# Second layer: values times keys as four matmuls of 32 by 32 in place of two of 64 by 64

## The chip, the cores and the metric

The kernel runs on one core of one Trainium2 chip. The metric is the device time of one execution in microseconds (us), and of several runs the median. Times of single instructions are in nanoseconds (ns).

## What is computed

Two layers of linear attention on x of shape (8, 512, 512), one after the other, each with its own weights. Cut to what matters, with H = 8 heads of 64 features in the first layer and H = 16 heads of 32 features in the second:

```
xn = layernorm(x)
q, k, v = xn @ Wq + bq, xn @ Wk + bk, xn @ Wv + bv      # masked by token
q = softmax(q, over the features of a head)
k = softmax(k, over the tokens)
attn = einsum('bhse,bhsd->bhed', k, v)                  # per head
y = einsum('bhtd,bhed->bhte', q, attn)                  # second layer
h = layernorm(y) * (1 + scale) + shift                  # scale, shift from silu(emb) @ W_emb
x = x + silu(h) @ W_out + b_out
```

(The first layer multiplies y the other way round, 'bnhd,bhdl->bnhl'.) The change touches the line of `attn`, in the second layer. Per batch entry and head it is a matrix of 32 by 32 there, summed over 512 tokens.

## The kernel before

**Units.** The work is cut into 16 units, one per layer and batch entry: units 0 to 7 are the first layer, 8 to 15 the second. Each unit has 512 tokens in four tiles of 128, and 512 features in four chunks of 128. Every product is made of float16 parts: a number is split into a high and a low part, and a product is high times high, high times low and low times high, so that each chunk of a sum is three matmuls (`split_pairs`).

**Order.** All orders are written out by hand, one list per engine, in functions `step(u)` for units 1 to 14 and `last_unit` for 15. TensorE does in unit u: keys K(u), values V(u), queries Q(u), each 48 matmuls of 512 columns (`project_keys`, `project_tokens`, all recorded at L534); then `attention(u)`, the product of values and keys (L658), into the PSUM bank `att_ps`; then the output projection of the unit before, `output(u - 1)`, 48 matmuls at L534; then `attend(u)`, queries times that product (L709), 96 matmuls. Unit 15 has the queries ahead of the values and the output tiles of unit 14 around `attention` and `attend`.

**The product of values and keys.** `attention(u)` walks over four chunks c of 128 features. A chunk holds two heads of the first layer or four of the second; heads don't mix, so of the 128 by 128 product of a chunk only blocks on the diagonal are wanted. `pairs_of_heads` makes, for each of the 12 pairs of operands (four token tiles by three parts), two matmuls: j = 0 takes the first 64 features of both operands and writes partitions 0 to 63, j = 1 the other 64 and partitions 64 to 127. That is 12 by 2 by 4 = 96 matmuls per unit, each with its weight load, all 128 rows deep. In the second layer a block of 64 by 64 holds two heads and, off its diagonal, two blocks of 32 by 32 that no head wants; `mask_attention` on DVE (L1089 in the second layer) multiplies by a table of blocks that is zero there, adding a value column first, and writes `att`. ACT and POOL split `att` into `att_hi` and `att_lo`, which `attend` reads.

**What waits for what around it.** TensorE starts `attention(u)` when the transposed keys, the low parts of the values and the gate of the unit before are ready. DVE does in unit u: four key tiles (`masked_keys`, L864 and L1021; L864 is a small memset that carries the wait for the tile) in between the work on the hidden rows of the unit before; low parts of keys; low parts of values (L1052); four query tiles (`queries`, L1072, L1075, L1077); `mask_attention`; sums; four residuals (L1120), each when an output tile is done; and the work on y (`attended_all`, L1130 to L1147), when `attend` has done two tiles. ACT takes the exponent of the queries (L1497) and their high part (L1504), POOL their low part (L1714).

**SP's queue.** SP issues the DMA transposes (L410), in this order in a unit: keys, h, the first half of the next unit's x, queries high and low (`turn_q`), the second half of the next unit's x (`turn_x(u, 1)`). `attend(u)` waits for the transposed queries, K(u + 1) for the transposed x. The queue is strictly in order.

Of the kernel before, what the change touches and what calls it, by code (L numbers as in the profile page):

```python
# [5 lines left out]
P = 128  # L6
# [10 lines left out]
HALF = P // 2  # L17
# [32 lines left out]
def layer_of(u):  # L50
    return u // B
# [55 lines left out]
def build(nc, x_d, emb_d, mask0_d, mask1_d, w_d, bias_d, wemb_d, cols_d, ident_d, blocks_d, out_d):  # L107
    with ExitStack() as ctx:
# [105 lines left out]
        def tile(buffer, a, b):  # L214
            return buffer[:, (4 * a + b) * P:(4 * a + b + 1) * P]
# [29 lines left out]
        def att_count(u):  # L245

            return C + u + (C - 1 if u == LAST else 0)
# [271 lines left out]
        def _(pe):  # L519
# [17 lines left out]
            def split_pairs(lhs_hi, lhs_lo, rhs_hi, rhs_lo):  # L537
                return [p for c in range(C) for p in ((lhs_hi(c), rhs_hi(c)), (lhs_hi(c), rhs_lo(c)), (lhs_lo(c), rhs_hi(c)))]
# [111 lines left out]
                    last = nc.tensor.matmul(out, ones[:], rows, start=True, stop=True)  # L650
                last.then_inc(shift_summed, 1)

            def pairs_of_heads(c, pairs):

                for n, (lhs, rhs) in enumerate(pairs):
                    for j in range(2):
                        g = slice(j * HALF, j * HALF + HALF)
                        last = nc.tensor.matmul(att_ps[g, c, g], lhs[:, g], rhs[:, g], start=(n == 0), stop=(n == len(pairs) - 1))  # L658
                return last

            def attention(u):
                pe.wait_ge(kt_hi_ready, 16 * (u + 1))
                pe.wait_ge(kt_lo_ready, 16 * (u + 1))
                pe.wait_ge(v_lo_ready, 4 * (u + 1))
                if u:
                    pe.wait_ge(att_ready, att_count(u - 1))
                if u == 2:
                    pe.wait_ge(film_copied, 4)
                for c in range(C):
                    f = slice(c * P, c * P + P)  # L670
                    k_parts = (lambda t: tile(kt_hi, c, t), lambda t: tile(kt_lo, c, t))
                    v_parts_t = (lambda t: v_hi[:, t, f], lambda t: v_lo[:, t, f])
                    left, right = (k_parts, v_parts_t) if layer_of(u) == 0 else (v_parts_t, k_parts)
                    last = pairs_of_heads(c, split_pairs(*left, *right))
                last.then_inc(att_summed, 1)

            def first_attention(between):
# [69 lines left out]
            def step(u):  # L747
# [34 lines left out]
                if shifted is not None:  # L782
                    pe.wait_ge(shift_folded, folded(1, shifted))
                pe.wait_ge(h_ready, 4 * u)
                attention(u)
                if u == 1:
                    pe.wait_ge(o0_ready, 1)
# [7 lines left out]
            def last_unit(u):  # L795
                pe.wait_ge(xt_hi_ready, 32 * u)
                pe.wait_ge(xt_lo_ready, 32 * u)
                project_keys(u)
                project_tokens("Q", u, Q_, xt_hi, xt_lo)
                project_tokens("V", u, V_, xt_hi, xt_lo)  # L800
                pe.wait_ge(ht_hi_ready, 16 * u)
                pe.wait_ge(ht_lo_ready, 16 * u)
                output(u - 1, (0,))
                pe.wait_ge(h_ready, 4 * u)
                attention(u)
                output(u - 1, (1,))
                attend(u)
                output(u - 1, (2, 3))
# [1043 lines left out]
```

## Time and profile before

| | |
|---|---|
| three runs | 805.05, 800.82, 802.58 us |
| median | 802.58 us |
| profiled execution, span from first to last instruction | 799.5 us |
| instructions in the trace | 16864 |
| DMA, mean over the span | 164 GB/s |

For the profiled execution no time of its own is given beside its span, so what lies around the span is taken from the median: 3.1 us. The profile is one execution. TensorE has two rows in it: PE is the matmuls, PEld the weight loads, which overlap them. A row such as "128*64 128x64 f16 x96" reads: weights of 128 rows by 64 columns, moving operand of 128 rows by 64 columns, float16, 96 of them merged. Matmuls are pipelined, so the duration of one (196 ns here) is not its cost: the cost is the distance from one start to the next. "issue" is time in which an engine waited for nothing that the profile shows; the landing of a DMA transpose is among what it does not show. SPq is the queue of SP: its rows give the time that issuing takes, not the landing.

### The profile page before, as it was taken

How to read it: one execution, taken by the hardware profiler on the slowest of the kernel's cores; microseconds unless marked ns; L12 is line 12 of the kernel's file. 1: busy time of each engine (PE TensorE's matmuls, PEld its weight loads, DVE VectorE, ACT ScalarE, POOL GpSimd, SP SyncE). 2: the span in 40 equal slices, each digit the busy share in tenths (PEclk: the TensorE clock that was granted, in tenths of full speed). 3: DMA queues.
4: the chain of work that ended last, by engine and by line, in shares of the span. 5: the costliest groups of instructions: out<-in, count | busy, mean ns of one | idle time of the engine just before them, and what ended most of it. 6: DMA issues, size and time to landing. Idle time of an engine off the chain costs nothing.

```text
span 799.5 us, 16864 instructions
## 1 busy us (share of the span) xinstructions
PE 761.5 (95%) x6359; PEld 370.6 (46%) x6359; DVE 697.7 (87%) x1427; ACT 517.5 (65%) x1011; POOL 438.5 (55%) x433
## 2 busy tenths in 40 slices
PE   5997999999999999998999999999999999999986
PEld 2445444454544445444444544444454544444442
DVE  7898978798998999999988898898888889888885
ACT  5896766666667686885856685665767575560633
POOL 2465573663737767486672755447364545546323
PEclk9997999999999999999999999999999999999999
DMA  9976895856939769595794939487684939477462
GB/s 327 297 142 183 253 184 176 158 139 162 182 128 158 198 137 201 134 200 148 137 220 87 204 93 180 151 159 198 99 198 113 190 123 185 112 139 153 80 132 80
DMA packets 291249, 130.73 MB, mean 164 GB/s; under 512 B 261440, under 2 KB 261824, under 8 KB 291168
## 3 DMA queue, kind: packets, MB, share of 16 engines
q1 hardware_dynamic: 288432, 125.27, 70.8%
q10 hardware_dynamic: 2736, 4.39, 1.5%
q8 instruction: 50, 0.82, 0.4%
q14 instruction: 31, 0.25, 0.1%
HBM read 47.74 MB, written 16.88 MB: 81 GB/s over the span
## 4 chain that ended last, share of the span: by engine, by line
PE 85%; DVE 9%; issue 3%; ACT 2%; DMA 0%; POOL 0%; SPq 0%; DVEq 0%; ACTq 0%; POOLq 0%
PE ring L534 75%; PE ring L709 3%; PE att_ps L658 3%; DVE sb_k_or_qt L1042 1%; DVE sb_row_peak L881 1%; ACT sb_k_or_qt L1440 1%; DVE sb_q_sum L1101 1%; PE ring L834 0%; PE att_ps L595 0%; PE film_ps L595 0%; DVE sb_q_max L1075 0%; DVE ring L1072 0%; DVE sb_ht_parts L1158 0%; PE film_ps L604 0%; DMA sb_x<-in_x 0%
## 5 line engine op out<-in xcount | busy, mean ns | idle before, releaser
L534 PE MATMUL ring<-sb_w_hi,sb_xt_parts 128*128 128x512 f16 x1024 | 309.0, 379 | 0.0
L534 PE MATMUL ring<-sb_w_lo,sb_xt_parts 128*128 128x512 f16 x512 | 194.0, 379 | 0.0
L534 PE MATMUL ring<-sb_w_hi,sb_ht_parts 128*128 128x512 f16 x512 | 155.8, 379 | 4.0 <-ACT sb_ht_parts L1610 1.4
L534 PEld LDWEIGHTS ring<-sb_w_hi,sb_xt_parts 128*128 128x128 f16 x1024 | 100.4, 98 | 126.0 <-issue 6.6
L534 PE MATMUL ring<-sb_xt_parts,sb_w_hi 128*128 128x512 f16 x496 | 148.6, 381 | 9.7 <-issue 9.1
L1698 POOL TENSOR_TENSOR sb_htok<-sb_ht_parts,sb_htok 128x512 f16<-128x512 f32 x60 | 75.0, 1272 | 137.8 <-ACT sb_htok L1473 137.8
L1714 POOL TENSOR_TENSOR sb_tanh<-sb_v_or_q,sb_kq_hi 128x512 f16<-128x512 f32 x64 | 74.1, 1159 | 87.7 <-ACT sb_kq_hi L1504 87.1
L534 PE MATMUL ring<-sb_w_lo,sb_ht_parts 128*128 128x512 f16 x256 | 97.0, 379 | 0.0
L534 PE MATMUL ring<-sb_xt_parts,sb_w_lo 128*128 128x512 f16 x248 | 94.5, 381 | 0.0
L1497 ACT ACTIVATE sb_v_or_q<-ring,sb_ln_one 128x512 f32<-128x512 f32 x64 | 43.9, 686 | 61.0 <-DVE ring L1077 60.9
L1689 POOL TENSOR_TENSOR sb_x<-sb_x,sb_bias_o 128x512 f32<-128x512 f32 x64 | 79.3, 1274 | 5.9 <-DVE sb_w_lo L958 5.9
L534 PEld LDWEIGHTS ring<-sb_w_hi,sb_ht_parts 128*128 128x128 f16 x512 | 50.1, 98 | 63.4 <-ACT sb_ht_parts L1610 4.1
L534 PEld LDWEIGHTS ring<-sb_xt_parts,sb_w_hi 128*128 128x128 f16 x496 | 47.5, 98 | 67.2 <-issue 12.3
L534 PEld LDWEIGHTS ring<-sb_w_lo,sb_xt_parts 128*128 128x128 f16 x512 | 50.1, 98 | 59.4 <-issue 0.7
L1709 POOL TENSOR_TENSOR sb_tok<-sb_v_or_q,sb_tok 128x512 f16<-128x512 f32 x56 | 66.4, 1199 | 17.1 <-ACT sb_tok L1436 17.1
L1417 ACT ACTIVATE sb_v_parts<-sb_x,sb_x_minus 128x512 f16<-128x512 f32 x52 | 36.9, 710 | 58.4 <-POOL sb_x_minus L1670 58.4
L1120 DVE SCALAR_TENSOR_TENSOR sb_x<-ring,sb_down_o,sb_x 128x512 f32<-128x512 f32 x60 | 43.2, 748 | 28.3 <-PE ring L534 26.0
L1042 DVE SCALAR_TENSOR_TENSOR sb_k_or_qt<-sb_k_or_qt,sb_k_recip,sb_kq_hi 128x512 f16<-128x512 f32 x64 | 61.5, 961 | 5.1
L1440 ACT ACTIVATE sb_k_or_qt<-sb_k_or_qt,sb_k_shift 128x512 f32<-128x512 f32 x64 | 45.4, 710 | 20.3 <-DVE sb_k_shift L1029 20.3
L1432 ACT ACTIVATE sb_v_or_q<-sb_x,sb_x_add,sb_x_rstd 128x512 f32<-128x512 f32 x56 | 43.9, 808 | 22.2 <-POOL sb_x_add L1677 22.2
L1464 ACT ACTIVATE att_ps<-sb_ht_parts,sb_scale_down 128x512 f32<-128x512 f32 x30 | 20.6, 687 | 57.6 <-DVE sb_ht_parts L1153 57.5
L1072 DVE SCALAR_TENSOR_TENSOR ring<-ring,sb_scale_down,sb_bias_q 128x512 f32<-128x512 f32 x64 | 48.0, 750 | 9.1 <-PE ring L534 9.0
(232 smaller groups left out, 1401.0 us busy)
## 6 DMA issues: line engine op xcount, KB each, us to landing
out<-sb_x SPq DMA_DIRECT2D x14, 1024.0 KB, 4.9
sb_rows_now<-film_rows SPq DMA_DIRECT2D x16, 512.0 KB, 4.5
sb_x<-out SPq DMA_DIRECT2D x8, 1024.0 KB, 5.2
sb_x<-in_x SPq DMA_DIRECT2D x7, 1024.0 KB, 5.4
sb_mask_add<-mask_terms SPq DMA_DIRECT2D x15, 256.0 KB, 5.5
sb_w_hi<-in_L_cond_W_emb SPq DMA_DIRECT2D x1, 1536.0 KB, 14.1
sb_w_lo<-in_L_cond_W_emb SPq DMA_DIRECT2D x1, 1536.0 KB, 14.4
sb_w_hi<-in_L_cond_film_emb_W ACTq DMA_DIRECT2D x1, 1536.0 KB, 11.9
```

The source lines that it names most:

```text
L534: last = nc.tensor.matmul(out, lhs, rhs, start=(n == 0), stop=(n == len(pairs) - 1))
L1042: nc.vector.scalar_tensor_tensor(out=k_lo[:, i * S:i * S + S], in0=k_or_qt[:, i, :], scalar=k_recip[:, i:i + 1], in1=kq_hi[:, i * S:i * S ...
L1072: nc.vector.scalar_tensor_tensor(out=here, in0=here, scalar=scale_down[:, layer, Q_:Q_ + 1], in1=bias_q[layer][:], op0=ALU.mult, op1=ALU.a ...
L1120: nc.vector.scalar_tensor_tensor(out=xt(unit, t), in0=bank("O", t, unit), scalar=down_o[:, layer:layer + 1], in1=xt(unit, t), op0=ALU.mult ...
L1417: nc.scalar.activation(unused(unit)[:, t, :], xt(unit, t), ACT.Square, bias=x_minus[:, t:t + 1], accum_out=x_square[:, t:t + 1]).then_inc( ...
L1432: nc.scalar.activation(xh_of(unit)[:, t, :], xt(unit, t), ACT.Identity, bias=x_add[:, t:t + 1], scale=x_rstd[:, t:t + 1]).then_inc(xh_read ...
L1440: nc.scalar.activation(k_or_qt[:, i, :], k_or_qt[:, i, :], ACT.Exp, bias=k_shift[:, i:i + 1], accum_out=k_sum[:, i:i + 1]).then_inc(k_exp, 1)
L1497: nc.scalar.activation(q[:, t, :], bank("Q", t, u), ACT.Exp, bias=ln_one[:]).then_inc(q_exp, 1)
L1689: nc.gpsimd.tensor_tensor(xt(u, t), xt(u, t), bias_o[layer][:], ALU.add).then_inc(x_biased, 1)
L1698: nc.gpsimd.tensor_tensor(hp_lo[:, t, :], y_of(unit)[:, t, :], hp_hi[:, t, :], ALU.subtract).then_inc(h_lo_ready, 1)
L1709: nc.gpsimd.tensor_tensor(xp_lo[:, t, :], xh_of(unit)[:, t, :], xp_hi[:, t, :], ALU.subtract).then_inc(xp_lo_ready, 1)
L1714: nc.gpsimd.tensor_tensor(q_lo[:, t * D:t * D + D], q[:, t, :], kq_hi[:, t * D:t * D + D], ALU.subtract).then_inc(q_lo_ready, 1)
```

## The change

In units 8 to 15 each group of two matmuls of 64 by 64 becomes a group of four matmuls of 32 by 32, one per head, in the four quarters of the array's columns, with outputs in the four quarters of the partitions. A unit's block has 12 by 4 by 4 = 192 matmuls and as many weight loads in place of 96. The blocks off the heads' diagonal are no longer written; the table of blocks zeroes them as before. Units 1 to 7 call the same function with two groups, and unit 0 has its own (`first_attention`). Nothing else changes: in the order of TensorE's instructions each row of 96 matmuls of 64 by 64 in units 8 to 15 is a row of 192 of 32 by 32 at the same place, with the same waits. The new function is one line longer, so that lines behind it have numbers higher by one in the changed kernel.

```diff
-            def pairs_of_heads(c, pairs):
-
+            def groups_of_features(c, groups, pairs):
+
+                width = P // groups
                 for n, (lhs, rhs) in enumerate(pairs):
-                    for j in range(2):
-                        g = slice(j * HALF, j * HALF + HALF)
+                    for j in range(groups):
+                        g = slice(j * width, j * width + width)
                         last = nc.tensor.matmul(att_ps[g, c, g], lhs[:, g], rhs[:, g], start=(n == 0), stop=(n == len(pairs) - 1))
                 return last
...
-                    last = pairs_of_heads(c, split_pairs(*left, *right))
+                    last = groups_of_features(c, 4 if layer_of(u) else 2, split_pairs(*left, *right))
```

## Rows read from the trace of the kernel before

**Rows 1.** The page: busy time by engine, and the ending chain by engine
```profile
PE 761.5 (95%) x6359; PEld 370.6 (46%) x6359; DVE 697.7 (87%) x1427; ACT 517.5 (65%) x1011; POOL 438.5 (55%) x433
...
PE 85%; DVE 9%; issue 3%; ACT 2%; DMA 0%; POOL 0%; SPq 0%; DVEq 0%; ACTq 0%; POOLq 0%
```

**Rows 2.** Chain of waits, units 8 to 15: start us, us, what
```profile
456.21 0.82 issue
457.03 31.24 PE ring L534 x144
...
502.55 1.01 issue
...
548.42 0.31 issue
...
593.58 0.49 issue
...
638.92 0.75 issue
...
684.53 0.12 issue
...
729.79 1.20 issue
...
769.82 1.67 issue
```

**Rows 3.** Stretches, L658 alone: length, PE, PEld, clock, DMA share, GB/s
```profile
442.53:444.17 1.64, 1.64 (x96) 1.59 (x96) 1.00 1.39 248
...
sum 13.12, PE 13.12 PEld 12.75; mean PE 1.64 PEld 1.59
```

**Rows 4.** PE in order, unit 8; first only up to 443.0 us
```profile
442.53 0.66 PE L658 MATMUL att_ps<-sb_kt_or_y,sb_v_parts 128*64 128x64 f16 x30
...
442.22 0.38 PE L534 MATMUL ring<-sb_w_hi,sb_xt_parts 128*128 128x512 f16 x1
442.53 1.71 PE L658 MATMUL att_ps<-sb_kt_or_y,sb_v_parts 128*64 128x64 f16 x96
...
445.26 0.59 PE L534 MATMUL ring<-sb_w_hi,sb_ht_parts 128*128 128x512 f16 x2
```

**Rows 5.** SP queue in order, transposes, units 9, 10, 11, 14
```profile
498.43 3.20 SPq L410 DMA_TRANSPOSE sb_xt_parts<-sb_tok  x2
...
543.60 3.19 SPq L410 DMA_TRANSPOSE sb_xt_parts<-sb_tok  x2
...
589.21 2.89 SPq L410 DMA_TRANSPOSE sb_xt_parts<-sb_tok  x2
...
725.70 3.18 SPq L410 DMA_TRANSPOSE sb_xt_parts<-sb_tok  x2
```

**Rows 6.** DVE in order: fourth key tile, units 9 to 15; L1089
```profile
467.69 0.06 DVE L864 MEMSET sb_spare<- 128x1 f32 x1 [0.91 <-PE ring L534]
...
491.69 1.12 DVE L1089 SCALAR_TENSOR_TENSOR sb_att<-att_ps,sb_v_column_up,sb_blocks 128x128 f32<-128x128 f32 x4
...
514.22 0.06 DVE L864 MEMSET sb_spare<- 128x1 f32 x1 [0.17 <-PE ring L534]
...
559.75 0.06 DVE L864 MEMSET sb_spare<- 128x1 f32 x1
...
605.22 0.06 DVE L864 MEMSET sb_spare<- 128x1 f32 x1
...
650.33 0.06 DVE L864 MEMSET sb_spare<- 128x1 f32 x1 [0.85 <-PE ring L534]
...
695.91 0.06 DVE L864 MEMSET sb_spare<- 128x1 f32 x1
...
741.64 0.06 DVE L864 MEMSET sb_spare<- 128x1 f32 x1 [0.71 <-PE ring L534]
```

**Rows 7.** The page, DMA queues: packets, MB, share of 16 engines
```profile
q8 instruction: 50, 0.82, 0.4%
```

## The prediction

> **What bounds the kernel now.** I read the page first [rows 1]: TensorE is busy 95% of the span and the chain that ended last lies on it for 85%, which looks as if every microsecond taken from it were a microsecond gained. The chain of waits of units 8 to 15 then corrects that [rows 2]. In each of units 8 to 14 TensorE stands still behind the last product of queries and attention (L709), before the next unit's keys: 0.82, 1.01, 0.31, 0.49, 0.75, 0.12 and 1.20 us, all "issue", a wait whose end the profile does not name. The queue of SP names it [rows 5]: the last pair of transposes of the next unit's x is issued until 501.63, 546.79, 592.10 and 728.88 us in units 9, 10, 11 and 14, and the next keys start at 503.56, 548.73, 594.07 and 730.99 (a piece of rows 2 plus its length), 1.93, 1.94, 1.97 and 2.11 us later. So the keys start when a transpose lands. These transposes stand on SP behind those of the queries, and those wait for DVE, ACT and POOL on the query tiles, which come from the Q projection ahead of the changed block. The block is no link of that chain.
>
> The block (L658) itself takes 1.64 us in each unit, 13.12 us for the eight units of the second layer [rows 3], at a granted clock of 1.00, the 2.4 GHz level. DVE takes its result (L1089) in unit 9 at 491.69 us [rows 6], 1.85 us after it is there (488.20 plus 1.64), because four query tiles stand ahead of it.
>
> There is a second way from the block to the end: block, output projection, L709, then DVE's work on y, behind which DVE takes the four key tiles of the next unit. The fourth tile of units 9 and 10 comes 10.66 us after the first key matmul (467.69 less 457.03, 514.22 less 503.56), and DVE waits for it 0.91 and 0.17 us; 0.85 in unit 13 and 0.71 in unit 15 [rows 6]. In units 11, 12 and 14 there is no wait: DVE starts at 559.75, 605.22 and 695.91 where the tile was there at 559.39, 604.73 and 695.31, so DVE is late by 0.36, 0.49 and 0.60 us. Only there does an earlier block help. DVE then runs on to the queries and so to SP's transposes, and its gain is kept to the end.
>
> **The change, part by part.** Units 0 to 7 keep their matmuls. In eight units a block of 96 matmuls (48 pairs of two 64 by 64) becomes one of 192 (48 groups of four 32 by 32), each with its weight load; waits, order and DMAs stay, apart from more instructions to fetch.
>
> Price of a group. In the block 66 matmuls take 1.71 less 0.66 us [rows 4], 15.9 ns each, 31.8 a pair. 64 columns at 2.4 GHz are 26.7 ns, which leaves 5.1, or 2.6 for each matmul. In the projections 144 matmuls of 512 columns take 31.24 us [rows 2], 217 ns each against 213 of columns, 3.6 each. No row has quarters of the columns with 32 moving columns. Bounds: 13.3 ns of columns and the same 5.1 give 18.4; two halves one behind the other, 63.6. Between them I take 13.3 and four times 2.6, 23.7 ns, since the pair of this line is the nearest row and already shows two matmuls that overlap. That is 8.1 ns a group and 48 groups: the block falls by 0.39 us, eight of them by 3.1 us.
>
> What of it counts. In units 8, 9, 12 and 14 the gain falls in front of units whose DVE waits for keys anyway (9, 10, 13, 15): nothing, TensorE's idle time grows. The blocks of units 10, 11 and 13 feed units 11, 12 and 14, where 0.36, 0.39 and 0.39 us count: 1.1 us. In unit 15 TensorE waits 1.67 us for the transposed queries ahead of the last L709 [rows 2], so a faster block there gives nothing. What is late next is in every unit the transpose of x.
>
> Here a rule of the Trainium skill speaks against the change: "TensorEngine Tiling (Array Packing)", Instruction Overhead, puts some 60 cycles on each matmul, so that fewer columns than that save nothing, and advises against cutting a dimension that is already small. The pairs do not contradict it if each tile of the array has this floor of its own; two matmuls in 31.8 ns do contradict one floor for all. The sum by it is a rival below.
>
> More instructions: q8 carries 0.82 MB in 50 packets [rows 7], which for 2 times 6359 instructions is 64 bytes each, 256 to a packet. 1536 more instructions in all are 768 more matmuls and as many loads: 0.1 MB and six packets, nothing for the DMA engines. A block is now 384 instructions and crosses at least one packet; cover is whatever is fetched ahead. I cost it at nothing; without cover it is a rival.
>
> Sum: the profiled span of 799.5 us less 1.1 is 798.4. The median of the runs shown lies 3.1 above this span, so 801.5 us. A measurement here can tell about 0.5%, 4 us, from no change.
>
> **Rivals.**
> 1. A floor per tile (the page's rule as a mechanism here): 60 of the 64 columns' time, 25 ns, and the same 5.1 make 30.1 ns a group, the block 0.08 us shorter, 0.24 us in three units: 802.3 us. For it: nothing in this trace streams fewer than 64 columns in f16. Against: nothing. 0.20.
> 2. No more than two matmuls overlap, so the rate of 15.9 ns for a matmul stays whatever its size: a group takes 63.6 ns and the block 1.53 us more. This is the rival on the other side. Unit by unit the delay is the larger of 1.53 less DVE's wait and 1.53 less TensorE's idle time: 0.71 (unit 9), 1.36, 1.53, 1.53, 0.78, 1.53, 0.82 (unit 15), together 8.3; the last block hides in 1.67. 810.9 us. In general the loss is seven times the growth of a block less 2.45 us, so it passes 4 us from 0.92 us a block on, a group of 51 ns. For it: 15.9 ns is the fastest rate of this line. Against: 26.7 of 31.8 ns are columns, so it is the columns that limit it. 0.09.
> 3. The instruction stream runs dry in the block: 384 instructions in 1.1 us against 192 in 1.6. A packet's time is 0.4% of 16 times 799.5 over 50, 1.0 us [rows 7]; a block longer by that on balance costs 7 less 2.45, 4.6 us: 807.2 us. Against: the bursts of today show no gap. 0.05.
> 4. Quarters do not overlap at all: four times 31.8, 127 ns; the block grows by 4.6 us, 29.6 us in seven units and 2.9 in the last: 835 us. 0.02.
> 5. The transposes follow TensorE after all, so that every unit passes the whole gain on, and a group takes 18.4 ns: eight times 0.64 us, 797.4 us. Against: the steady 1.9 to 2.1 us from SP's last issue to the keys. 0.04.
>
> **How the numbers follow.** The forecast has 0.60. It and rival 1 lie within 0.5%: 0.80. Slower by over 0.5% are rivals 2 to 4: 0.16; faster rival 5: 0.04. The range runs from 799.0 (the forecast, the runs' spread, no group below 18.4 ns) to 807.5 and takes in rival 3; left out are rivals 2, 4 and 5, 0.15.
>
> **What would show it.** Right: the stretch of L658 in units 8 to 15 is 1.2 to 1.3 us, rows of 192; the idle time ahead of the keys of units 9, 10, 13 and 15 grows by 0.3 to 0.4 us; SP's last issue is still 1.9 to 2.1 us ahead of the keys; DVE's lateness in units 11, 12 and 14 is gone or below 0.3. Wrong: a block at or above 1.6 us (rival 1 where it is 1.55, rivals 2 or 4 at 3.2 or 6), single gaps in the block beside a q8 packet (rival 3), or keys that start earlier against Q's end in every unit (rival 5).

## The result and the profile after

The changed kernel takes 822.41 us, median of five runs (819.56 to 824.34), against 802.58 us (800.82 to 805.05): the ratio is 1.0256, with a 95% interval of 1.0239 to 1.0273. It is 20 us slower, where 801.5 was forecast. Its profiled execution took 820.82 us, with a span of 819.0 us; before, the span was 799.5.

The page of the changed kernel, against [rows 1] and [rows 7]:

```profile
PE 768.9 (94%) x7127; PEld 372.2 (45%) x7127; DVE 697.7 (85%) x1427; ACT 517.8 (63%) x1011; POOL 438.1 (53%) x433
...
q8 instruction: 56, 0.92, 0.5%
...
PE 78%; DVE 12%; issue 5%; ACT 3%; DMA 0%; POOL 0%; DVEq 0%; SPq 0%; ACTq 0%; POOLq 0%
```

DVE, ACT and POOL do the same work in a longer span. There are 768 more matmuls and six more instruction packets, as counted ahead. In the chain "issue" rises from 3 to 5%. The chain of waits by time shows where it stands now, against [rows 2] (start us, us, what):

```profile
442.45 1.32 PE att_ps L659 x138
443.78 0.21 issue
443.99 0.57 PE att_ps L659 x54
...
487.79 1.60 PE att_ps L659 x167
489.40 4.02 issue
493.42 0.37 PE att_ps L659 x13
493.79 12.74 PE ring L534 x48
506.52 1.51 PE ring L710 x96
508.03 31.19 PE ring L534 x144
...
541.07 0.54 PE ring L534 x2
541.61 3.13 issue
...
587.51 1.79 PE att_ps L659 x192
589.30 10.47 PE ring L534 x48
...
681.70 2.95 issue
...
685.11 12.15 PE ring L534 x48
...
731.79 3.56 issue
...
735.62 12.99 PE ring L534 x48
```

The idle time ahead of the keys is gone in five of seven units (506.52 plus 1.51 is the start of the keys, 508.03). In its place TensorE stands still inside the block in units 8, 9, 13 and 14, two matmuls behind it in unit 10 and five behind it in unit 15, for up to 4 us, and the wait has no releaser in the profile. In unit 11 the same 192 matmuls pass without a stop.

The same places in TensorE's timeline, unit 9 and then unit 11:

```profile
487.72 1.68 PE L659 MATMUL att_ps<-sb_kt_or_y,sb_v_parts 128*32 128x32 f16 x167
493.42 0.37 PE L659 MATMUL att_ps<-sb_kt_or_y,sb_v_parts 128*32 128x32 f16 x25 [4.02 <-issue]
...
587.45 1.85 PE L659 MATMUL att_ps<-sb_kt_or_y,sb_v_parts 128*32 128x32 f16 x192
```

**What the stops have in common.** I numbered the records of TensorE's instructions in order of time, from the first one on. The first instruction behind each long stop has the number 193 or 194 modulo 256: in units 8, 9, 13 and 14 in the block, in units 10 and 15 a few matmuls behind it. A q8 packet is 0.92 MB over 56, 16.4 KB, 256 instructions of 64 bytes. So a stop lies at the edge of a packet. In the second layer the first edge inside a block comes at instruction 22, 79, 135, 192, 249, 50, 107 and 139 of the block in units 8 to 15, since a unit is 967 instructions long there, 57 short of four packets. The stop is always at the second edge, 256 instructions on. That fits a stream that can be two packets ahead, where the refill that starts at one edge must be there by the next.

| unit | first edge at | stop, us | from first edge to going on, us |
|---|---|---|---|
| 8 | 22 | 0.40 | 1.5 |
| 9 | 79 | 4.20 | 5.4 |
| 10 | 135 | 3.51 | 5.1 |
| 11, 12 | 192, 249 | none | |
| 13 | 50 | 3.14 | 4.3 |
| 14 | 107 | 3.74 | 5.1 |
| 15 | 139 | 2.28 | 4.4 |

(Here a stop is counted from one matmul's start to the next, 17.3 us in all.) A block of 384 instructions takes 1.7 us from its first matmul to its last where it does not stop (unit 11; 1.5 us before), and outruns the refill; one of 192 cannot hold two edges. In unit 8 the packet was under way 0.8 us ahead of the edge, while TensorE was still at the long matmuls in front of the block: I read this as the sequencer fetching ahead of the array. In the other units of the table the packet starts 1.8 to 3.1 us after the edge, takes 0.9 to 1.2 us, and TensorE goes on 1.4 us after its end.

A part of this price may belong to the DMA transposes. Around every block SP issues transposes: `turn_x` in units 9 to 14, those of the queries in unit 15. With them in flight the packets in the blocks start 1.8 to 3.1 us after the edge. Six other edges of the changed kernel in units 8 to 14 lie in the rows of L710, and there the packet starts 0.5 to 0.8 us after the edge, in four of them with no transpose packet in flight and in two with some. No run takes the transposes away, so what part of the price is theirs stays open.

The Trainium skill ("Runtime: NRT & Kernel Launch", Instruction fetch mechanics) has refills of 16 KiB, 256 instructions, into a memory of two such lines, and holds the fetch to be hidden since dispatch is slower than the refill. The trace agrees with the size and with two lines; here dispatch (256 instructions in about 1 us) was the faster one. The same section also gives TensorE 128 KiB, 2048 instructions, and with these stops the trace does not agree.

**The clock.** The stretches of unit 9 (length, PE, PEld, DVE, ACT, POOL busy, granted clock, DMA share, GB/s):

```profile
493.60:498.20 4.60, 4.60 (x36) 1.72 (x23) 4.26 (x10) 3.08 (x9) 3.13 (x4) 0.50 1.17 160
498.30:506.50 8.20, 8.20 (x42) 3.58 (x41) 2.71 (x5) 2.93 (x8) 5.00 (x7) 1.00 0.57 116
```

The granted clock falls inside the stop of 4.20 us, at 491.5, and is 0.50, the 1.2 GHz level, until 498.2, and then 1.00 again. The output projection takes 12.74 us in unit 9, 12.15 in unit 13 and 12.99 in unit 14 in place of 10.47. In unit 10, after a stop of 3.51 us, it did not fall. The lower clock adds 6.5 us to these three output projections.

**The sum of unit 9 closes.** Keys start later than before by -0.48, 4.47, 7.60, 8.30, 9.35, 14.12 and 19.12 us in units 9 to 15 (456.55 less 457.03, 508.03 less 503.56 and so on). The step of 4.95 us in unit 9 is: block and stop 6.00 in place of 1.64, 4.36; slower output tiles, 2.27; less the idle time of 0.60 ahead of L709 and of 1.01 ahead of the keys, both used up: 5.0.

Units 11 and 12 have no stop, and yet the keys behind them are a further 0.70 and 1.05 us late. For unit 12 the trace names a second way in which a refill costs time. Before, the transposes of x land 1.8 to 2.0 us after SP's last issue (the semaphore's times in the trace). SP's rows at the end of unit 12 are now:

```profile
642.70 2.78 SPq L410 DMA_TRANSPOSE sb_xt_parts<-sb_tok  x2
646.96 0.39 SPq L490 DMA_DIRECT2D out<-sb_x  x1
```

The last issue ends at 645.47, an instruction packet runs from 646.73 to 647.69, the transposes land at 648.93, 3.5 us after the issue, and the keys start at 649.02. Over all the kernels run here, nine of these landings ahead of the keys of units 9 to 15 took 3.1 to 3.6 us, and each of the nine had an instruction packet that started 0.6 to 1.5 us after SP's last issue. The other landings took at most 2.5 us, and four of them had such a packet too. So a packet seems able to hold a transpose up, but need not; no run was made for it.

### The profile page after: what moved, and what is told of

Its sections match the earlier page's. It is cut to its first block, busy times and chain, and to the rows that moved or that the text cites. A ratio compares the mean times of both kernels' runs of the same rounds, so it can differ in the third digit from the quotient of the medians.

```text
span 819.0 us, 18400 instructions
## 1 busy us (share of the span) xinstructions
PE 768.9 (94%) x7127; PEld 372.2 (45%) x7127; DVE 697.7 (85%) x1427; ACT 517.8 (63%) x1011; POOL 438.1 (53%) x433
## 4 chain that ended last, share of the span: by engine, by line
PE 78%; DVE 12%; issue 5%; ACT 3%; DMA 0%; POOL 0%; DVEq 0%; SPq 0%; ACTq 0%; POOLq 0%
PE ring L534 69%; PE att_ps L659 3%; PE ring L710 3%; DVE sb_k_or_qt L1043 1%; DVE sb_row_peak L882 1%; ACT sb_k_or_qt L1441 1%; DVE sb_q_sum L1102 1%; DVE sb_x L1121 1%; ACT sb_v_or_q L1488 1%; DVE ring L1131 1%; DVE sb_y_stats L1135 1%; DVE sb_ht_parts L1159 1%; ACT sb_v_parts L1490 1%; DVE ring L1073 1%; DVE sb_q_max L1076 1%
## 5 line engine op out<-in xcount | busy, mean ns | idle before, releaser
L534 PE MATMUL ring<-sb_w_hi,sb_ht_parts 128*128 128x512 f16 x512 | 160.6, 389 | 9.0 <-issue 6.1
L534 PE MATMUL ring<-sb_w_lo,sb_ht_parts 128*128 128x512 f16 x256 | 99.6, 389 | 0.0
```

Of the source, the lines that this page charges most:

```text
L534: last = nc.tensor.matmul(out, lhs, rhs, start=(n == 0), stop=(n == len(pairs) - 1))
```

## Experiments

**Shift the stream by 100 instructions.** Matmuls of 32 by 32 into the first bank of the keys, ahead of the keys of unit 8, 50 of them with their loads. Only the place of the packet edges changes for units 9 to 15.

```diff
+            def pad_keys(u, count):
+                out = take_bank("K", 0, u)
+                lhs, rhs = w_hi[1][K_][:, 0, 0:32], w_hi[1][K_][:, 1, 0:32]
+                for n in range(count):
+                    nc.tensor.matmul(out[0:32, 0:32], lhs, rhs, start=True, stop=True)
...
+                if u == B:
+                    pe.wait_ge(w_ready[1], 2)
+                    pad_keys(u, 50)
```

> Edit: the changed kernel, with 50 matmuls of 32 by 32 ahead of the keys of unit 8, into a bank that the keys then overwrite: 100 instructions more, once. Instructions come in packets of 256, and in the changed kernel the first packet edge inside a block of 384 lies at instruction 21, 76, 133, 190, 247, 48, 105, 138 of the block in units 8 to 15 (counted in the trace). Theory 'stream runs dry': TensorE stops where a second edge follows within some 5 us, that is where the first edge lies below about 140. Shifted by 100 the edges lie at 177, 232, 33, 90, 147, 204, 5, 38: long gaps (over 0.3 us) go from units 9 and 13 and appear in unit 11 (3 to 4.5 us); unit 10 shows a shorter one (0.4 to 3), unit 14 next to none, unit 15 one of 1 to 3. Time about 812 to 817 us. Rival 'quarters stall by themselves' (by place in the program or by their operands): the gaps stay in units 9, 10, 13 and 14, and the time is that of the changed kernel and 1.5 us, 822 to 826.

Measured: 815.67 us, ratio 1.0189 (1.0153 to 1.0226). TensorE's timeline, unit 9 and unit 11:

```profile
488.52 2.25 PE L665 MATMUL att_ps<-sb_kt_or_y,sb_v_parts 128*32 128x32 f16 x192
...
581.69 1.69 PE L665 MATMUL att_ps<-sb_kt_or_y,sb_v_parts 128*32 128x32 f16 x173
586.71 0.32 PE L665 MATMUL att_ps<-sb_kt_or_y,sb_v_parts 128*32 128x32 f16 x19 [3.32 <-issue]
```

The two units have changed places: unit 9 passes, unit 11 stops for 3.5 us at its instruction 347, where the edge was to lie. Units 13 and 14 have no long stop, unit 10 one of 0.8, unit 12 one of 1.5 us behind the block (edge at 148, which I had counted out), unit 15 one of 3.7, more than expected. The same instructions with the same operands stop or pass by their number alone.

**Keep the edge in a harmless place.** The same padding, 38 matmuls ahead of the keys of unit 8 and 29 ahead of those of each later unit, so that a unit is some 1024 instructions long.

> Edit: the changed kernel with 38 small matmuls ahead of the keys of unit 8 and 29 ahead of those of each unit 9 to 15, so that a unit is 1024 or 1025 instructions long and the packet edge stays at about instruction 200 of each block (170 in unit 15). Theory 'stream runs dry': no gap over 0.3 us in or behind any block, no fall of the granted clock, and a time of 802 to 806 us, since the added 0.5 us per unit lies mostly in the idle time ahead of the keys. Rival 'quarters stall by themselves': 820 to 828 us.

Measured: 805.7 us, ratio 1.0072 (1.0047 to 1.0096). The waits of TensorE in units 8 to 14 have one row left:

```profile
PE ring L716 <- issue: 0.4, 1, 0.4
```

and its chain of waits shows what the padding costs in each unit, here of units 10 and 11:

```profile
536.78 10.47 PE ring L534 x48
547.25 1.51 PE ring L716 x96
548.75 0.82 PE ring L657 x29
549.57 31.18 PE ring L534 x144
```

No stop, no slow output tile, all 1536 quarter matmuls still there, and some 15 of the 20 us are back (the ratio falls from 1.0256 to 1.0072). The 0.82 us of padding lie where TensorE idled before, and in four units they are more than that idle time, by 1.6 us together. The profiled execution agrees: its last keys come 1.7 us later than before. But it is the fastest of four, 803.49 us; the median is 5 us above before (4 to 8), and what the rest of these 5 us is stays open. It is still slower than the kernel before, and so no version to take.

**The old tiles, twice.** 384 instructions in a block, and no quarter among them: each chunk's 24 matmuls are issued twice.

```diff
-                    last = pairs_of_heads(c, split_pairs(*left, *right))
+                    for again in range(2 if layer_of(u) else 1):
+                        last = pairs_of_heads(c, split_pairs(*left, *right))
```

> Edit: the kernel before, with the 24 matmuls of each chunk issued twice in the second layer (the second time overwrites the first): 384 instructions in a block, all of the old 64 by 64 kind. The packet edges lie as in the changed kernel, but 256 instructions last 2.0 us in place of 1.0. 'Stream runs dry': gaps in or just behind the blocks of units 9, 10, 13, 14 and 15, each about 1 us shorter than in the changed kernel (2 to 3.3 us), and with the block 1.5 us longer a time of 822 to 830 us. Rival 'only quarters': no gap, and 1.0% above before.

Measured: 820.12 us, ratio 1.0248 (1.0227 to 1.0268), somewhat below the range expected. Unit 9:

```profile
489.19 2.85 PE L658 MATMUL att_ps<-sb_kt_or_y,sb_v_parts 128*64 128x64 f16 x167
495.01 0.60 PE L658 MATMUL att_ps<-sb_kt_or_y,sb_v_parts 128*64 128x64 f16 x25 [2.98 <-issue]
```

It stops at the same matmul as the changed kernel, the 168th. Stops of 3.18, 2.24, 2.00, 2.37 and 0.95 us in units 9, 10, 13, 14 and 15, 1.0 to 1.4 us shorter than there, since 256 instructions last 1 us longer here, I take it. So the stops need no quarter tile.

**Cut the moving columns, not the weights.** The kernel before, with its 64 moving columns in two matmuls of 32 (184 matmuls in a block):

```diff
+                    for i in range(1 if n == 0 else 2):
...
+                            r = g if n == 0 else slice(j * HALF + i * 32, j * HALF + i * 32 + 32)
+                            last = nc.tensor.matmul(att_ps[g, c, r], lhs[:, g], rhs[:, r], start=(n == 0), stop=(n == len(pairs) - 1 and i == 1))
```

> Edit: the kernel before, tiles of 64 as before, but after the first of the 12 pairs of operands the 64 moving columns are cut in two matmuls of 32: 184 matmuls and loads in a block in place of 96, with no quarter tile anywhere. Group price: with a floor of 25 to 31 ns per tile the block is about 2.8 us, with a rate of 7.9 ns per matmul about 1.5 us. 'Stream runs dry': a unit is 951 instructions, the first edges lie at 21, 94, 167, 240, 57, 130, 203, 252, so gaps in units 9, 12 and 13 (1.5 to 4 us each, 1 us shorter where the block is slower) and 808 to 818 us. 'Quarters stall by themselves': no gap, and 801 to 804 us, or 810 with the slower block.

Measured: 821.38 us, ratio 1.0261 (1.0230 to 1.0291). A unit without a stop (unit 10):

```profile
540.00 3.09 PE L659 MATMUL att_ps<-sb_kt_or_y,sb_v_parts 128*64 128x64 f16 x184
```

The block is 3.1 us, so two matmuls of 32 columns on one tile of 64 cost as much as two of 64, as the floor has it (2.8 expected). Stops of 3.9 and 2.6 us in units 9 and 12, as placed; in unit 13 only 0.6, and one of 3.0 in unit 15 that I had not expected. There the stop comes at instruction 251 of the block, and the edge before it lies some five instructions ahead of the block; from that edge to the stop TensorE needed only 3.1 us. The time is above what either theory gave. The block is 1.4 us longer, by the prediction's count worth 7.4 us, and the granted clock was 0.50 for 3.4 us at each of the three long stops; I put the excess down to these two, and neither was run apart.

**What a group costs.** Three runs leave heads out.

Changed kernel, two of the four quarters (`for j in (0, 2)`):

> Edit: the changed kernel, but of the four heads of a chunk only the first and the third are made (the product of values and keys of the other two is left out in the second layer): 96 matmuls of 32 by 32 in a block. It prices the group. If 31.6 ns is a floor of each tile, a pair of quarters costs 31.6 too and the block stays at 1.51 us; if it is a rate of 7.9 ns for each matmul with its load, the pair costs 15.8 and the block is 0.76 us; if it is a rate with columns on top, between. With 192 instructions in a block no two packet edges fall into it: 'stream runs dry' expects no long gap and 800 to 804 us; 'quarters stall by themselves' expects gaps and over 810 us.

Measured: 801.66 us, ratio 1.0013 (1.0001 to 1.0025). Unit 11:

```profile
581.11 1.37 PE L659 MATMUL att_ps<-sb_kt_or_y,sb_v_parts 128*32 128x32 f16 x96
```

Kernel before, the first half only (`for j in (0,)`):

> Edit: the kernel before, but in the second layer only the first of the two halves of a chunk is made (the product of values and keys of the other two heads is left out): 48 matmuls of 64 by 64 in a block. The prices of a group so far: two tiles of 64, 31.6 ns, with 64 or with 32 moving columns; four tiles of 32, 31.6; two tiles of 32, 25. Theory 'weight loads in sum': a group pays for the columns of weights of all its tiles, 128 in the first three, with a floor of 25 ns; a single tile of 64 then costs 25 ns and the block is 1.2 us. Theory 'each tile pays for its own load of 64' (and the four quarters are bound by another thing, 7.9 ns a matmul): 31.6 ns and 1.5 us.

Measured: 803.32 us (one run, 800.58 before). Unit 11:

```profile
581.32 1.71 PE L658 MATMUL att_ps<-sb_kt_or_y,sb_v_parts 128*64 128x64 f16 x48
```

From the first start to the last the block of pairs of quarters takes 1.19 us, 25 ns a pair, and that of lone halves 1.51, as long as that of two halves [rows 4], 32 ns. The sum of weight columns (25 ns for a lone half) falls: a tile of 64 columns costs 32 ns by itself, and a second one beside it nothing. Two of 32 columns side by side cost 25 ns; a lone one was not run. Four quarters, in the changed kernel's stretches without a stop, take about 32 ns (31.2 to 32.8 from block to block), 8 for each matmul with its load.

The run of lone halves took 2.7 us more than before with a block that is no longer. A part of that may be the transposes of x, which land 3.2 and 3.5 us after SP's last issue at the ends of units 10 and 13, each time with an instruction packet in between.

Changed kernel, three of the four quarters:

> Edit: the changed kernel, but of the four heads of a chunk only the first three are made (the product of the fourth is left out in the second layer): 144 matmuls of 32 by 32 in a block, 288 instructions. The lone tile of 64 has shown 31.6 ns, so a tile of 64 pays that by itself and a tile of 32 about 25. What bounds the group of four at 31.6? Theory 'rate': 7.9 ns for each matmul with its load, so three cost 23.7, less than the 25 of a tile: the block is 1.2 us. Theory 'four quarters cost what 128 columns of weights cost': three cost between, 28 to 29 ns and 1.35 us. For 'stream runs dry' a unit is 871 instructions and the first edges lie at about 21, 175, 72, 225, 122, 19, 172, 45 or so: a gap in or just behind the blocks of units 10, 12 and 15 of 2 to 4.5 us, short ones in 8 and 13, and 806 to 816 us.

Measured: 805.11 us (one run, 800.54 before). Unit 14:

```profile
715.27 1.45 PE L659 MATMUL att_ps<-sb_kt_or_y,sb_v_parts 128*32 128x32 f16 x144
```

The fastest blocks take 1.26 to 1.27 us from first to last start, 26.5 ns a group, with a short pause of 0.06 us or more in each; from one group to the next it is mostly 25 ns. That is what the rate gives (23.7, but not below the 25 of a pair), and below 28 to 29. I had misjudged unit 10, which stops for 0.4 us only: with 288 instructions in a block the second edge comes 38 instructions, some 4 us, into the output tiles. Unit 12 shows no stop in or right behind its block either, unit 8 one of 0.5 and unit 15 one of 2.8; the keys of unit 15 come late too, with the transposes landing 3.6 us after SP's last issue. That the group of four is bound by a rate of instructions is the better reading, not a shown one.

**Spread the block.** The changed kernel with chunk 0 behind the second query tile, chunk 1 behind the third, chunks 2 and 3 behind the fourth:

```diff
+                    if u >= B and i:
+                        if i == 1:
+                            attention_waits(u)
+                        attention_chunks(u, ((0,), (1,), (2, 3))[i - 1])
...
-                attention(u)
+                if u < B:
+                    pe.wait_ge(h_ready, 4 * u)
+                    attention(u)
```

> Edit: the changed kernel, with the block of units 8 to 14 cut in three: chunk 0 behind the second query tile, chunk 1 behind the third, chunks 2 and 3 behind the fourth; unit 15 keeps its block. The same 192 quarter matmuls with the same operands, 256 instructions spread over 3.5 to 7 us instead of 1 to 2. 'Stream runs dry' (a refill takes 4.3 to 5.4 us from a packet edge): gaps of 0.3 to 1.8 us in units 9, 10 and 14, none in 8, 11, 12 and 13, and 804 to 808 us. 'Quarters are slow by themselves': 820 or more.

Measured: 804.63 us, ratio 1.0055 (1.0038 to 1.0071). The chain of waits of unit 9:

```profile
482.52 0.56 issue
483.08 0.53 PE att_ps L659 x48
483.61 2.70 PE ring L534 x12
486.30 0.46 PE att_ps L659 x48
486.76 2.70 PE ring L534 x12
489.46 0.98 PE att_ps L659 x96
490.45 10.52 PE ring L534 x48
```

The same quarter matmuls at the same price, thinned by query tiles: no stop at an edge in any of units 8 to 14, not even the short ones that I expected in 9, 10 and 14, and one of 2.3 us in unit 15, which kept its block. What is left of the loss is in part the new waits for the first chunk (0.56 us here), and in part longer idle time ahead of the keys of units 12 and 13, 1.8 and 1.9 us from one start to the next in place of 0.7 and 0.9, where the transposes of x land 2.5 and 3.2 us after SP's last issue.

**A longer block without more packets.** The kernel before, with 7 more matmuls of 512 columns behind each block.

```diff
+            def pad_output(u, i):
+                out = take_bank("O", i, u - 1)
+                for n in range(7):
+                    nc.tensor.matmul(out, ht_hi[:, i, 0, :], w_hi[1][Q_][:, 0, :], start=True, stop=True)
```

> Edit: the kernel before, with 7 matmuls of 512 columns more (1.52 us, 14 instructions) between the block of each unit 8 to 15 and the output tile behind it, into that tile's bank. It measures what a longer block costs where nothing runs dry. Theory of the prediction: TensorE's idle time and DVE's waits absorb part, the loss is seven times 1.52 less 2.45, 8.2 us, a time 1.0% above before. Rival 'nothing is absorbed': eight times 1.52, 12.2 us, 1.5%. Rival 'the transposes alone bound it': under 3 us.

Measured: 806.72 us, ratio 1.0079 (1.0064 to 1.0094), 6.3 us. The chain in unit 8:

```profile
442.70 1.64 PE att_ps L663 x96
444.34 1.62 PE ring L656 x7
445.95 10.36 PE ring L534 x48
456.31 1.51 PE ring L714 x96
457.82 7.89 PE ring L534 x36
```

Of 12.2 us added about half is absorbed. The unit-by-unit count of the prediction gave 8.2, 2 us too high; the measured 6.3 us lie between the two rivals.

## Why the prediction was wrong, point by point

- **"Only there does an earlier block help" and what is absorbed.** Right in its kind. A block 0.3 us shorter (two of four quarters) gave no gain, ratio 1.0013; with a block in effect 1.5 us longer about half of that reached the end (6.3 of 12.2 us). The gain of 1.1 us that I forecast was not seen in any run, and it had no ground, since the block did not get shorter: 1.7 us in unit 11 against 1.5 before, from first to last matmul.
- **"I take 13.3 and four times 2.6, 23.7 ns."** Wrong: about 32 ns, no less than the pair of halves. I had split the pair's 31.8 ns into columns and a fixed part for each matmul. But the lone half costs 32 ns too, and a pair of halves costs no less with 32 moving columns than with 64, so the price is that of a tile and hardly depends on the moving columns; "it is the columns that limit it", in rival 2, falls with this too. Rival 1, with 30.1 ns, was closer. Two quarters side by side cost 25 ns, three hardly more, and the fourth brings it to 32. The floor of 60 cycles that the Trainium skill gives ("TensorEngine Tiling (Array Packing)", Instruction Overhead) would be 25 ns by my estimate at 2.4 GHz; the pair of quarters agrees with it, and the tile of 64 with 32 moving columns, at 32 ns, lies above it.
- **"More instructions ... I cost it at nothing; without cover it is a rival."** This is the step that failed. I put the fetch of 1536 more instructions at nothing; it cost stops of 17.3 us in all and 6.5 us of lower clock, part of which idle time absorbed. Cover was one packet. I had the packet's size, the 384 instructions in a block and the 1 us that they need, and took the absence of gaps today as evidence. It was none: with 192 instructions a block cannot hold two edges, so the trace of before could not show it.
- **Rival 3** had the mechanism and missed the price: 1.0 us is the packet's own time, but from the edge to going on it is 4 to 5.5 us here (3.9 to 5.9 in all the kernels that stop, where the packet was not under way at the edge). It also had no second effect, the clock at 1.2 GHz behind a stop, worth 6.5 us. It gave 807.2, with 1.0 us more in every block, where 822.4 was measured, with five stops of 2.3 to 4.2 us in eight units. The sign that I had named for it, single gaps beside a q8 packet, is what came. 0.05 was far too low a chance.
- **Rival 2** was wrong as a mechanism: four quarters do overlap.
- **The range** left out 0.15 of the chances that I had written down; the size of the fetch's price had no upper end in it at all. The packet's time was a lower bound, not an estimate.

## What to carry to other kernels

Count instructions, not only matmuls: cutting a matmul into smaller tiles multiplies matmuls and loads, and in these runs a burst that ran through 256 of them in less than the refill's 4 to 5 us stopped at the second packet edge, with either size of tile, unless the packet was already under way. The 4 to 5 us were taken with transposes in flight; a kernel without them may have a shorter refill. Whether a burst stops depends on its place modulo 256, so test by shifting the stream. Long matmuls between thinned such a burst enough here. Price a tile by a run of that tile alone: two halves were already side by side at the price of one, and four quarters cost the same.

## What the runs showed that I had not expected

- TensorE's refill: packets of 256 instructions, 1.1 to 3.8 us from an edge to the packet's start, 0.9 to 1.3 us of transfer, and 1.2 to 2.1 us until the next matmul. An instruction packet between SP's last issue and the landing of the transposes of x went with a landing 1.1 to 1.8 us later than usual in nine cases.
- The stop is at the instruction 194 modulo 256, within an instruction or two, in all six kernels that stop. A stop that the profile calls "issue" can be found by counting.
- Tiles of 128 rows by 64 columns cost 32 ns each time: in pairs with 32 or 64 moving columns, and alone with 64. Two tiles of 32 columns side by side cost 25 ns, four of them 32.
- The granted clock fell to 0.50 behind stops of 4.20, 3.14 and 3.74 us in the changed kernel, for 3.4 to 6.8 us, and not behind one of 3.51 us. With the old tiles twice it fell behind stops of 2.24 and 2.37 us and not behind one of 3.18, so the length of a stop alone does not decide it.
